# Where the own query-key product stands in a one-core graph attention kernel: from VectorE to GpSimd for ten pair batches

## The reference, cut to what matters

```python
mask = adj + eye(n)                       # n = 4096, adj sparse, some rows far denser than others
q, k, v = (h @ Wq.T + bq), (h @ Wk.T + bk), (h @ Wv.T + bv)   # 8 heads of 32
scores = einsum('nhd,mhd->hnm', q, k) / sqrt(32)
scores = where(mask == 0, -1e9, scores)
attn = softmax(scores, axis=-1)
ctx = einsum('hnm,mhd->nhd', attn, v).reshape(n, 256)
h1 = layer_norm(h + ctx @ Wo.T + bo, ln1_g, ln1_b)
h2 = layer_norm(h1 + relu(h1 @ W1.T + b1) @ W2.T + b2, ln2_g, ln2_b)
```

## Time and profile before

| | |
|---|---|
| median of three runs | 561.72 us |
| profiled execution | 560.06 us, its span 558.2 us |
| PE busy | 482.2 us (86%) |
| DVE busy | 431.7 us (77%) |
| POOL busy | 266.3 us (48%) |
| ACT busy | 211.3 us (38%) |
| chain that ended last | PE 35%, DVE 30%, DMA 15%, issue 10%, POOL 5% |

### The profile page before, as it was taken

The page is one execution under the profiler, slowest core; times in us unless marked ns, Lnnn a source line. Parts: engine busy times, 40 slices in busy tenths (PEclk is TensorE's granted clock), DMA queues, the critical chain, the costliest instruction groups (busy, mean ns, idle before and its releaser), DMA issues.

```text
span 558.2 us, 7295 instructions
## 1 busy us (share of the span) xinstructions
PE 482.2 (86%) x2274; PEld 376.0 (67%) x2274; DVE 431.7 (77%) x1002; ACT 211.3 (38%) x513; POOL 266.3 (48%) x381
## 2 busy tenths in 40 slices
PE   5999998966798999798988899979878798789994
PEld 4888897855447747664775487468645687458883
DVE  0758697998799999999998899797998898661103
ACT  1233342324452362345235333633633233532430
POOL 6444357353633557457745244534455635305133
PEclk9999998999699999999999899998979699899998
DMA  8999869999989599788969774626658832401011
GB/s 287 417 420 416 307 223 345 410 406 425 351 325 374 182 388 326 286 306 312 341 238 326 240 284 159 253 60 247 210 197 276 296 110 85 134 28 39 1 39 42
DMA packets 39771, 141.07 MB, mean 253 GB/s; under 512 B 4904, under 2 KB 16424, under 8 KB 35632
## 3 DMA queue, kind: packets, MB, share of 16 engines
q1 hardware_dynamic: 24608, 95.17, 45.2%
q0 software_dynamic: 13328, 43.55, 23.1%
q10 hardware_dynamic: 1792, 1.85, 1.0%
HBM read 123.74 MB, written 16.80 MB: 252 GB/s over the span
## 4 chain that ended last, share of the span: by engine, by line
PE 35%; DVE 30%; DMA 15%; issue 10%; POOL 5%; ACT 4%; POOLq 0%; SPq 0%; ACTq 0%; DVEq 0%
PE ps L1690 10%; DVE found L500 10%; DMA work<-q_table,row_of 7%; PE ps L1061 7%; PE ps L1074 6%; PE ps L1041 4%; DMA xT_all<-in_xT 4%; DVE stats L1128 2%; DVE slots L602 2%; POOL slots L989 2%; DMA adj_buf<-in_adj 2%; DVE s_edge L590 1%; PE ps L827 1%; DVE work L587 1%; PE ps L1029 1%
## 5 line engine op out<-in xcount | busy, mean ns | idle before, releaser
L500 DVE FIND_INDEX8 found<-ones,adj_buf 128x8 uint32<-128x4105 int32 (+5 forms) x40 | 138.7, 3467 | 0.0
L1074 PE MATMUL ps<-w,xT_all 128*128 128x256 f32 x512 | 121.2, 392 | 2.6 <-ACT xT_all L1108 1.3
L1061 PE MATMUL ps<-xT_all,w 128*128 128x512 f32 (+1 forms) x288 | 122.8, 573 | 0.3 <-ACT xT_all L1091 0.2
L1074 PEld LDWEIGHTS ps<-w,xT_all 128*128 128x128 f32 x512 | 98.0, 196 | 16.2 <-ACT xT_all L1108 1.6
L1061 PEld LDWEIGHTS ps<-xT_all,w 128*128 128x128 f32 x288 | 54.8, 199 | 45.1 <-issue 42.1
L989 POOL DMA_INDIRECT slots<-kv_table,col_of x54 | 58.6, 1085 | 45.9 <-ACT row_of L896 16.6
L1108 ACT ACTIVATE xT_all<-ps,col_table 128x512 f32<-128x512 f32 (+1 forms) x72 | 45.8, 642 | 54.8 <-PE ps L1061 47.0
L1690 PE MATMUL ps<-early,xT_all 128*128 128x256 f32 x256 | 60.2, 398 | 5.8 <-DMA early<-in_wqkvT 5.8
L1690 PEld LDWEIGHTS ps<-early,xT_all 128*128 128x128 f32 x256 | 50.8, 200 | 13.9 <-DMA xT_all<-in_xT 4.8
L1128 DVE BATCH_NORM_STATS2 stats<-ps 128x6 f32<-128x256 f32 x62 | 22.2, 418 | 41.3 <-PE ps L1029 41.3
L979 POOL DMA_INDIRECT slots<-kv_table,found x32 | 38.2, 1193 | 28.3 <-PE ps L830 13.5
(11 more groups left out here) (176 smaller groups left out, 819.5 us busy)
## 6 DMA issues: line engine op xcount, KB each, us to landing
adj_buf<-in_adj SPq DMA_DIRECT2D x31, 2048.0 KB
xT_all<-in_xT SPq DMA_DIRECT2D x14, 512.0 KB, 24.9
kv_table<-slots POOLq DMA_DIRECT2D x7, 1024.0 KB, 11.2
slots<-kv_table SPq DMA_DIRECT2D x12, 512.0 KB
q_table<-slots POOLq DMA_DIRECT2D x16, 256.0 KB, 9.9
out_dram<-early SPq DMA_DIRECT2D x7, 512.0 KB
q_own<-q_table SPq DMA_DIRECT2D x12, 256.0 KB
slots<-in_adj SPq DMA_DIRECT2D x1, 2048.0 KB, 23.3
```

The costliest lines, as they stand in the source:

```text
L500: last = nc.vector.max_index(dst, ones8[:], part)
L1061: last = nc.tensor.matmul(ps[:, q["bank"] + f % 2, 0:q["g"] * P], w1[:, k, f * P:(f + 1) * P], q["h1T"][:, k, :], start=(k == 0), stop=(k ...
L1074: nc.tensor.matmul(to, q["ffT"][:, f, j * P:(j + 1) * P], w2[:, f, :], start=(f == 0), stop=False)
```

## The change

`own_scores_dve` is split. For the batches of steps 1 to 10 (`by_pool`) the product is now one GpSimd instruction, placed at the end of the step before, behind a wait for that step's edge values to be weighted, the last VectorE work ahead of the second search. VectorE keeps the sum and waits for the product. Batches 0, 11 and 12 to 18 keep the product on VectorE. A job's scale and shift are now always in two steps: scale in steps 5, 7 and 9 right behind the product, shift in steps 6 and 8 right behind the product, in step 10 ahead of the edge gathers. The store follows the shift, so it too is issued one step later (steps 6, 8 and 10). The counter `edge_probs` becomes a part of `edge_weighted`.

```diff
+        def two_searches(i):
+            return i + 2 < NB and STEPS[i + 2].T > 1
+        def by_pool(q):
+            return q.b >= 1 and q.T > 1 and two_searches(q.b - 1)
+        def own_product_pool(pool, q):
+            own_rows_ready(pool, q)
+            nc.gpsimd.tensor_tensor(own_keys(q), own_keys(q), own_queries(q), ALU.mult).then_inc(own_product, 1)
+
         def own_scores_dve(dve, q):
...
+            keys = own_keys(q)
+            if not by_pool(q):
+                own_rows_ready(dve, q)
+                nc.vector.tensor_tensor(keys, keys, own_queries(q), ALU.mult).then_inc(own_product, 1)
+            dve.wait_ge(own_product, q.b + 1)
             wait(dve, own_weighted, q.b)
...
-        def apart(q):
-            return step_of_job(q)[1] == 1 and finished(q) >= 0 and q.b + 2 < NB and STEPS[q.b + 2].T == 1
+        def scaled(q):
+
+            return step_of_job(q)[1] == 1 and finished(q) >= 0 and q.b + 2 < NB
...
-                if i >= 1 and apart(STEPS[i - 1]):
+                if i >= 1 and scaled(STEPS[i - 1]):
                     m = finished(STEPS[i - 1])
                     post_store(sp, JOBS[m], m, JOBS[m]["t"])
...
+                def scale_and_shift():
+
+                    if i >= 1 and scaled(STEPS[i - 1]):
+                        post_pool_final(pool, JOBS[finished(STEPS[i - 1])], finished(STEPS[i - 1]))
+                    if scaled(q):
+                        pool.wait_ge(s_weights, 16 * WEIGHT_DMAS)
+                        post_pool_gain(pool, JOBS[n - 1], n - 1)
+
+                if not two_searches(i) and (scaled(q) or i >= 1 and scaled(STEPS[i - 1])):
                     pool.wait_ge(own_probs, i + 1)
...
+                    scale_and_shift()
                 if soon:
                     gather_edges(pool, soon)
...
-                if place == 1 and n >= 1 and not apart(q) and i + 2 < NB:
-                    pool.wait_ge(edge_weighted, i + 1)
-                    pool.wait_ge(s_weights, 16 * WEIGHT_DMAS)
-                    post_pool_gain(pool, JOBS[n - 1], n - 1)
-                    post_pool_final(pool, JOBS[n - 1], n - 1)
+                if two_searches(i):
+                    pool.wait_ge(edge_weighted, 2 * i + 2)
+                    own_product_pool(pool, soon)
+                    scale_and_shift()
```

More of the change, by code:

```diff
@@ L328, in build @@
         ell_taken = sem("ell_taken")
+        own_product = sem("own_product")
         own_scores = sem("own_scores")
@@ L338, in build @@
         edge_exp = sem("edge_exp")
-        edge_probs = sem("edge_probs")
         own_weighted = sem("own_weighted")
@@ L596, in edge_scores_dve, with own_keys, own_queries, own_rows_ready @@
                                     ).then_inc(spread_ready, 1)
-        def own_scores_dve(dve, q):
[L599 to L604, removed]
+        def own_keys(q):
+            return slots[q.par][:, 0:q.T * q.own, 0:D].rearrange("p (t s) d -> p t s d", t=q.T)
+        def own_queries(q):
+            return q_own[q.par][:, 0:q.T, :].unsqueeze(2).to_broadcast([P, q.T, q.own, D])
+        def own_rows_ready(eng, q):
+            eng.wait_ge(own_loaded[q.par], total_par(lambda p: 2, q) * 16)
+            wait(eng, got_aligned[q.par], total_par(lambda p: p.U * p.A, q) * 16)
+        def two_searches(i):
[5 more added lines that the diff above has]
+            nc.gpsimd.tensor_tensor(own_keys(q), own_keys(q), own_queries(q), ALU.mult).then_inc(own_product, 1)
+        def own_scores_dve(dve, q):
+            keys = own_keys(q)
[3 more added lines that the diff above has]
+            dve.wait_ge(own_product, q.b + 1)
             wait(dve, own_weighted, q.b)
@@ L618, in masked_dve @@
             dve.wait_ge(mask_ready, q.p + 1)
-            dve.wait_ge(own_scores, 2 * q.b + 2)
+            dve.wait_ge(own_scores, q.b + 1)
             if q.A:
@@ L688, in edge_weight_dve @@
             p = p_edge[:, 0:q.U, :]
-            nc.vector.scalar_tensor_tensor(p, p, 1.0, tr_out(q)[:, :, HEADS:], ALU.min, ALU.mult).then_inc(edge_probs, 1)
-            dve.wait_ge(edge_probs, q.b + 1)
+            nc.vector.scalar_tensor_tensor(p, p, 1.0, tr_out(q)[:, :, HEADS:], ALU.min, ALU.mult).then_inc(edge_weighted, 1)
+            dve.wait_ge(edge_weighted, 2 * q.b + 1)
             v = edge_slots(q)[:, :, D:].rearrange("p u (h d) -> p u h d", d=DK)
@@ L806, in tr_pe @@
             pe.wait_ge(recip_ready, q.b + 1)
-            wait(pe, edge_probs, q.b)
+            wait(pe, edge_weighted, 2 * q.b)
             for u in range(q.U):
@@ L812, in sum_pe @@
         def sum_pe(pe, q):
-            pe.wait_ge(edge_weighted, q.b + 1)
+            pe.wait_ge(edge_weighted, 2 * q.b + 2)
             pe.wait_ge(own_weighted, q.b + 1)
@@ L1430, in _ @@
                     post_load(sp, JOBS[GROUPS], 0, JOBS[GROUPS]["t"])
-                if i >= 1 and apart(STEPS[i - 1]):
+                if i >= 1 and scaled(STEPS[i - 1]):
                     m = finished(STEPS[i - 1])
                     post_store(sp, JOBS[m], m, JOBS[m]["t"])
-                if place == 1 and n >= 1 and not apart(q):
+                if place == 1 and n >= 1 and not scaled(q):
                     post_store(sp, JOBS[n - 1], n - 1, JOBS[n - 1]["t"])
```

6 lines of the change are left out of this document (removed).

## The result

The changed kernel takes 567.9 us (median of 4 runs, 566.3 to 569.0), the kernel before 561.2 us beside it: a ratio of 1.0108, 95% interval 1.0065 to 1.0151. It is slower by 1.1%; forecast were 566.5 us and a range of 557 to 575, with "no change" (0.48) put a little ahead of "slower" (0.40). The profiled execution took 568.47 us, its span is 566.8 us, against 560.06 and 558.2 before: 8.4 us more, where the sum of the prediction had 4.8.

What follows compares the result with a forecast made beforehand. TensorE waits before its lists for VectorE's L550, which stands behind the own product and its sum. Losses 2.2 + 9.8 + 0.5 less the gain 7.7 give +4.8 us on the median 561.72: 566.5 us, range 557 to 575.

Steps and rivals of the forecast that it cites:

- Rival 1: GpSimd does not hold up VectorE's two-operand instructions; sum -3.7 us, 558.0 us; chance 0.2.
- (a): Steps 0 to 2: GpSimd's products of batches 1 and 2 come too late for VectorE's sum; loss 2.2 us.
- (c): Steps 4 to 8: GpSimd work outlasts the second search and holds up VectorE's next instructions; losses 9.8 us.
- sign (a): Step 2: GpSimd's product of batch 2 starts after 130 us and VectorE is idle before its sum.
- The 0.4 us of cover: Step 2: TensorE's attention matmuls, ending just before L789, hide some 0.4 us of a 2.6 us lateness.
- the input gathers of step 8 cover 2.35 us: Step 8: 2.35 us of waiting for a transfer were free, leaving a loss of 2.3 us.
- (d): Steps 7 and 9: ScalarE's write of `out` waits for the later store, taken as 7 us; loss 0.5 us together.
- Rival 3: Store lands 12 us or more after issue; some 5 us more in steps 7 and 9 each, 576 us; chance 0.18.
- The gain of 7.7 us: Steps 4 to 9: product leaves VectorE, worth the smaller of product and TensorE's idle time; 7.7 us together.

Runs made afterwards that it cites:

- e4: The changed kernel, all ten products on GpSimd, but a job's scale and shift together in the odd steps behind the product; ratio 1.0072 to the kernel before.
- e8: The changed kernel with shift and store early in even steps, and copies (batches 5, 9) and a memset (batch 7) replacing products; ratio 0.9918.
- e1: The changed kernel with the products of batches 1 and 2 back on VectorE; ratio 1.0032 to the kernel before.
- e13: The changed kernel with 16 filler matmuls, output unread, in TensorE's idle time in step 2; ratio 1.0059 to the kernel before.
- e3: The changed kernel with all own products on VectorE, scale and shift still split with the late shift; ratio 1.0064 to the kernel before.
- e7: The changed kernel with no product on GpSimd and the shift and store early in steps 6, 8 and 10; ratio 0.9945 to the kernel before.
- e9: The changed kernel with products 1 and 2 back on VectorE and shift and store early in the even steps; 556.5 us, ratio 0.9902.
- e2: The changed kernel with the product of batch 2 alone back on VectorE; ratio 1.0025 to the kernel before.

## Why the prediction was right, and where its sum was off

- **Right: the sign**, and the mechanism: GpSimd's instructions hold up VectorE behind a search. The bound taken for two-operand instructions, GpSimd's full length, is what the rows show (L537 2.97 us, L534 2.26 in e4). Rival 1, which needed the opposite, is out. The Trainium skill ("SBUF — State Buffer", "SBUF: two separate sides") has the same bound, an exclusive lock for the whole instruction that whichever starts first gets. The trace agrees on the length, but by its records not always on who wins: L537 begins 0.57 us before the product and is held all the same. The Trainium skill excepts there a VectorE instruction with two SBUF inputs beside a GpSimd instruction that does not read SBUF; no run here tried that pair, since in e8 the memset met a cast.
- **The size was less exact than 566.5 against 567.9 looks.** The sum had +4.8 us. The ratio makes it 6.1 us, and step 18 of the profiled execution begins 8.8 us late: 4.8, plus 2.2 in (a) and 1.9 in step 9, less 0.9 in (c), plus 0.8 behind step 10, where nothing was forecast. That the two medians lie 1.4 us apart is in part luck.
- **(a) was mis-sized**: 2.2 us forecast, 4.4 in the trace, 4.3 by e1. The prediction let the product start after 130 us and the sum wait for it. ScalarE's copy came 2.2 us earlier, the product ran at 128.20 and held L537, four instructions ahead of the sum, so sign (a) of the prediction did not show. The sum itself came only 1.0 us late (132.15 against 131.16); TensorE, whose L822 waits for L594, idled for 4.68 us, started 2.2 us late and went on at the lower clock. The step was priced on VectorE alone; half of the loss was TensorE's clock (2.2 us of 4.4, from L822 to the lists; with filler, in e13, that stretch is back to 2.7 us). The 0.4 us of cover was not there: L550 was done at 133.75, and the lists came at 137.70 for TensorE's sake.
- **(c) held**, and in its places: per step, with the gains, forecast +0.3, +0.5, +2.85, -0.6, +0.55 for steps 4 to 8 (3.6 together), measured -0.2, +0.2, +2.4, -0.3, +0.6 (2.7). The cast and not L534 took the wait in both steps, since it is the first one held. That the input gathers of step 8 cover 2.35 us was right: two casts of 5.0 us cost 2.4 and 0.6.
- **(d) was the right wait, mis-sized by its place**: 0.5 us for steps 7 and 9 together; ScalarE waited 0 us in step 7 and 3.32 in step 9, where the forecast had a gain of 1.0 and 0.9 was lost. The store took 9.2 us from issue to landing against the 7 assumed. Its price shows when less hides it: 4.84 and 8.00 us of waiting in e3. Rival 3, a landing after 12 us or more, did not come in the changed kernel, but did in e3 (12.40 us).
- **The gain of 7.7 us** cannot be read off one run. With the shift early, products 3 to 10 are worth 2.4 us net (e7 to e9, at the edge of what can be told), after casts of 1.3 to 2.7 us. TensorE's idle time before the lists was the right cap: it went to 0 in steps 5, 7 and 9, as said.
- What was not in the prediction: the costs overlap. Held VectorE instructions hide part of the wait for the store, 0 and 3.32 us in the changed kernel against 4.84 and 8.00 in e3. The times fit (the split alone costs 3.6 us, the products alone 4.0, both together 6.1), but the 1.5 us by which 6.1 is less than the sum cannot be told from nothing.

## What to carry to other kernels

Before work is given to GpSimd beside VectorE, look for a stretch in which VectorE sits in one long instruction or waits for another engine, and let it end inside; what outlasts it is added to VectorE's next small instructions, and is free only as far as VectorE would have waited for something else anyway (casts of 5.0 us cost 2.4 us in step 6 and 0.6 in step 8, each with the gain of a product in it). When a step is moved later, follow its output too: by the steps that became shorter, the store behind the shift cost more than the shift itself without products (7.1 us against 1.2, e3 to e7), and about as much with them (5.0 against 4.4). Where an engine is made to wait in front of TensorE, count TensorE's clock after the gap as well.

## What the runs showed of the hardware

- A GpSimd memset of 2.67 us, and copies, hold a VectorE cast up until they end, just as a two-operand multiply does.
- Not every small VectorE instruction is held: in e4 L526 and L528, 0.17 us each, ran from 226.29 on beside the shift that began at 226.29, and L534 behind them was held. L528 reads one operand and L534 two; L526 reads two as well, but its record begins with the shift's. What sets them apart is not shown.
- The held instructions have records that begin before GpSimd's: L537 at 127.63 for a product at 128.20, L594 at 130.58 for one at 131.00 (e13). At their usual 0.17 and 0.28 us they would have been over by then. Ahead of the product GpSimd was issuing a store (0.72 us), but the store alone does not hold VectorE: in e2, which has no product behind it, L537 took 0.17 us from 127.40 on, inside the store's 0.73 us from 127.22 on. Why the hold begins ahead of the product's record is open.
- GpSimd instructions with no semaphore between them leave the waiting cast no gap (5.00 us for two); with one between them the cast gets in after the first (e4).
- The granted clock was 0.63 in the window of 130 to 135 us, in which an idle time of 4.68 us ended, and the four matmuls behind it took 2.03 us; with 16 filler matmuls in the gap they took 1.09.
- It works the other way too, on gathers: in the kernel before, a gather issue of GpSimd that takes 0.95 us took 2.21 us at 224.17 and 2.20 at 239.41. Each began 0.4 us behind a VectorE multiply of 1.75 us (L602 at 223.81, L670 at 239.04) and ended 0.8 us behind its end. With the own product gone from VectorE, the first of the two takes 0.95 us (227.63 in the changed kernel).
